# Adding the last chunk's window sums part by part, with parts of 6, 6 and 1 tiles

## The chip, the cores and the metric

The kernel runs on one core of one Trainium2 chip. The metric is the device time of one execution in microseconds (us). Before the change the median of three runs is 8771.89 us (8764.04 to 8781.84).

## The reference

Four graph layers are applied one after the other to 6250 nodes with 128 features. The graph has 206250 edges, sorted by target. Each layer ends in `x = layernorm(x + layer(x))`. Cut to what matters here:

```python
# layer 0: an MLP on each edge, mean over the edges of a target
messages = relu(concat(x[src], x[dst], edge_attr) @ W1 + b1) @ W2 + b2
agg = segment_sum(messages, dst) / clip(counts, 1)

# layers 1, 2, 3: attention over the edges of a target
e = leaky_relu(a_s[src] + a_d[dst], 0.2)
p = exp(e - segment_max(e, dst)[dst])
z = segment_sum(p, dst)
out = segment_sum(h[src] * (p / z[dst]), dst)
# 1: self loops added, skip product, an inner layernorm; 2: plain
# 3: batch norm over all nodes, relu, residual
```

## The kernel before

**Tiles and chunks.** Edges are cut into tiles of 128 and chunks of K = 13 tiles; there are CH = 124 chunks, taken in 62 pairs with two buffers. A layer is an edge stage (all chunks) and then a node stage (13 blocks of up to 512 nodes), which writes the table of rows that the next layer gathers. After the last edge stage comes a final stage of two passes with the batch norm between them.

**A chunk, engine by engine.** Each engine has its own instruction order, written out by hand, with semaphores between them.

- GpSimd (POOL) issues 13 indirect DMAs (L563), one per tile, that gather source rows into `G`. It runs up to two chunks ahead: the gathers of chunk c+2 need the messages of chunk c, since they reuse its buffer.
- VectorE (DVE) starts its part of chunk c with `make_membership` for chunk c+1 (L1172): 0/1 matrices `memb` that say which edge of a tile has which target, formed in three instructions, for the tiles of `PARTED = [(0, 6), (6, 11), (11, 13)]`. Part p waits until TensorE has finished the window sums of the same part of chunk c-1, whose `memb` buffer it overwrites (`summed[p]`). Then, in an attention layer, come a forward scan for segment maxima (L1283, needs the gathered scores through TensorE's L763), window numbers loaded into registers, `keep_factor` (L1232), a backward scan (L1289), `rescale` of the accumulator (L1240, L1242), and the additions of chunk c-1's seven groups of window sums into `acc` (`add_sums`, L1252) in three batches: groups 0 to 2, then 3 and 4 behind L1320, then 5 and 6 behind L1341. Between them lie the carries (L1299 to L1307), the factor (L1313 to L1320), the maxima (L1326, L1328), the softened scores (L1337) and the difference (L1339). The last instruction is the message product (L1345).
- ScalarE (ACT) copies scores (L921), turned membership and so on, and takes the exponential of the difference (L989).
- TensorE (PE) turns `memb` of the next chunk (L699), forms the scores of the next chunk (L756, its first 8 tiles between the carries L777 and the transposition of weights L787, the rest after it), and at the end of the chunk the window sums (L709): for each of 13 tiles one product `memb` x `msg`, two tiles to a group, two TensorE instructions to a product. In layer 1 it also turns the first maxima (L785), which ScalarE copies ahead of the exponential.

In layer 0 a chunk has only the membership, the seven additions, and four additions of pre-activations to gathered rows (L1265); ScalarE applies the relu.

**The end of a layer.** The last chunk has no next membership. `finish_edges` waits for all its sums, rescales and adds the seven groups. TensorE, ScalarE, GpSimd and SyncE (SP) wait for the last of these additions before their node stage. SP's queue then issues, in this order, three loads of node rows (L454), the first two chunks' indices and marks of the next layer (L374, L424, L426), and in layer 0 the store and the reload of the flags of nodes with edges (L491, L493), which TensorE multiplies in L821. The node rows lie in `memb`'s memory.

**Node stages.** VectorE's order is by slots t = -3 to 16; a step with lateness d works on block t-d. In layer 2's node stage and in the final stage the sums of weights are inverted first, for all 49 tiles of nodes at once, 8 heads each (`inverse_weights`: two additions L1395 and L1396, a clamp L1447 or L1449, a reciprocal L1450); each block then uses its share (L1400, L1401, L1456). Layer 1's node stage does a like thing in the two parts of `PARTS`: 16 tiles of nodes first and 33 at slot 1 (`own_scores`, `own_shares`, with the reciprocal L1439).

Of the kernel before, what the change touches and what calls it, by code (L numbers as in the profile page):

```python
# [5 lines left out]
def gnn_program(nc, A, out):  # L6
# [13 lines left out]
    ALU = mybir.AluOpType  # L20
# [26 lines left out]
    HALF = 8  # L47
    PARTED = [(0, 6), (6, 11), (11, K)]
    BIG = float(2 ** 100)
# [7 lines left out]
    with ctx:  # L57
# [286 lines left out]
        def past(l, c):  # L344

            return 2 + CH * l + c
# [7 lines left out]
        def _(sp):  # L354
# [119 lines left out]
            def node_stage(l):  # L474
                sp.wait_ge(added[GR - 1], past(l, CH - 1))
                if l == 0:
# [52 lines left out]
        def _(pool):  # L529
# [91 lines left out]
            for l in range(4):  # L621
                if l:
                    pool.wait_ge(added[GR - 1], past(l - 1, CH - 1))
                    node_stage(l - 1)
                    for r in range(2):
                        pool.wait_ge(stored[r], 16 * len(range(r, NS * l, 2)))
                    for r in range(3):
                        pool.wait_ge(xnew_stored[r], 16 * len(range(r, NS * min(l, 2), 3)))
                else:
                    for k in range(4):  # L630
                        pool.wait_ge(row0_stored[k], 16 * len(range(k, NS, 4)))
                for b in range(2):
                    edges(l, b, b, 0, early=True)
                with pool.Fori(0, PAIRS - 1) as i:
                    for b in range(2):
                        edges(l, 2 * i + 2 + b, b, i + 1)
# [497 lines left out]
        def _(dve):  # L1134
# [140 lines left out]
            def attention(l, c, b, h, prev=True, ahead=True):  # L1275
# [14 lines left out]
                if prev:  # L1290
                    dve.wait_ge(summed[2], past(l, c - 1))
                    rescale(l, c - 1, win)
                    add_sums(l, c - 1, win, 0, 3)

# [26 lines left out]
                if prev:  # L1321
                    add_sums(l, c - 1, win, 3, 5)

# [18 lines left out]
                if prev:  # L1342
                    add_sums(l, c - 1, win, 5, GR)
                dve.wait_ge(wgt_turned, gpast(l, c))
# [11 lines left out]
            def finish_edges(l):  # L1356
                win = window_numbers(CH - 1)
                dve.wait_ge(summed[2], past(l, CH - 1))
                if l:
                    keep_factor(l, CH - 1)  # L1360
                    rescale(l, CH - 1, win)
                add_sums(l, CH - 1, win, 0, GR)
                dve.wait_ge(added[GR - 1], past(l, CH - 1))
# [3 lines left out]
            def then(ins):  # L1367
                count[0] += 1
                ins.then_inc(nvec, 1)
                dve.wait_ge(nvec, count[0])  # L1370
# [33 lines left out]
            def by_head(a):  # L1404
                return a.rearrange("p (j h) -> p j h", h=H)
# [37 lines left out]

            def inverse_weights(add, least):
                all_sums(by_head(zsum), F, 0, NBLK, FW)
                if add:
                    then(ts(zsum, zsum, add, least, ALU.add, ALU.max))  # L1447
                else:
                    then(ts(zsum, zsum, least, None, ALU.max))  # L1449
                then(nc.vector.reciprocal(zsum, zsum))  # L1450

# [71 lines left out]
            def node_stage(l):  # L1523
# [5 lines left out]
                if l == 2:  # L1529
                    inverse_weights(0, 1e-30)  # L1530
                for t in SLOTS:
                    if l == 1 and t == 1:
                        own_scores(1)
                        own_shares(1)
                    s = at(t, 0)
                    g = NS * l + t
# [65 lines left out]

            inverse_weights(1e-16, 1e-30)
            for t in SLOTS:
                s = at(t, -2)
                if s is not None:
# [80 lines left out]
```

## Time and profile before

| | |
|---|---|
| median of 3 runs | 8771.89 us |
| the profiled execution | 8773.27 us |
| its span (first to last instruction) | 8771.2 us |
| TensorE / VectorE / ScalarE / GpSimd busy | 73% / 59% / 24% / 71% of the span |
| granted TensorE clock, mean | 0.828 |
| HBM | 598.03 MB read, 26.58 MB written, 71 GB/s |

The edge stage of layer 0 runs up to 2132 us, that of layer 1 from 2267 to 4363, of layer 2 from 4511 to 6557 and of layer 3 from 6642 to 8688; the node stages lie between them. In the rows, names in brackets after "idle before" say what ended an idle time. "Busy" of TensorE is that of its products; its weight loads (PEld) run beside them. A clock of 1.00 is 2.4 GHz, 0.50 is 1.2 GHz.

### The profile page before, as it was taken

The page shows a single profiled execution, that of the slowest core. Times are in us where ns is not written, and L with a number is a line of the kernel's source. Part 1 is how long each engine was busy: PE and PEld are TensorE (multiplying, and loading weights), DVE is VectorE, ACT ScalarE, POOL GpSimd, SP SyncE. Part 2 cuts the span into 40 slices and gives each one's busy share as a digit, 9 for nine tenths or more (in the row PEclk, how much of TensorE's full clock was granted, in tenths as well). Part 3 has the DMA queues.
Part 4 walks back from the last instruction along what each step waited for, and adds up shares of the span by engine and source line. Part 5 has one row for each costly group of instructions (what it writes and reads, how often), then busy time and mean ns, then how long its engine had stood idle before and what let it go on. Part 6 is the DMA issues. An engine that isn't in the chain of part 4 may idle for free.

```text
span 8771.2 us, 141279 instructions
## 1 busy us (share of the span) xinstructions
PE 6428.0 (73%) x41611; PEld 5776.8 (66%) x41612; DVE 5143.8 (59%) x13620; ACT 2062.1 (24%) x7255; POOL 6267.6 (71%) x6594
## 2 busy tenths in 40 slices
PE   5777777777677777777777777777766777777775
PEld 4777777776566666666656666666655666666664
DVE  3333333334766666666676666666666666666666
ACT  2222222222322222222132222222222222222222
POOL 4777777776677777777657777777765777777774
PEclk7888888888888888888768888888877888888886
DMA  3333333332322222222232222222222222222222
GB/s 101 78 80 78 80 78 80 78 80 66 77 68 68 68 67 66 67 67 68 65 80 69 69 70 69 70 69 70 69 62 73 69 69 69 69 69 69 69 70 50
DMA packets 425473, 625.68 MB, mean 71 GB/s; under 512 B 189634, under 2 KB 305617, under 8 KB 425293
## 3 DMA queue, kind: packets, MB, share of 16 engines
q0 software_dynamic: 206336, 462.61, 22.5%
q1 hardware_dynamic: 219086, 162.49, 7.0%
q8 instruction: 20, 0.33, 0.0%
q14 instruction: 31, 0.25, 0.0%
HBM read 598.03 MB, written 26.58 MB: 71 GB/s over the span
## 4 chain that ended last, share of the span: by engine, by line
POOL 42%; issue 23%; PE 16%; DVE 11%; DMA 4%; DVEq 2%; SPq 1%; ACT 1%; POOLq 0%; ACTq 0%
POOL G L563 41%; PE ps L756 6%; PE ps L709 5%; DMA G<-rows,idx 3%; DVE msg L1345 2%; DVE acc L1252 2%; DVEq L1226 1%; DVE memb L1172 1%; PE ps L728 1%; PE ps L731 1%; PE ps L777 1%; DVE acc L1242 1%; DVE shared L1299 1%; DVE shared L1307 1%; DMA idx<-in_src 1%
## 5 line engine op out<-in xcount | busy, mean ns | idle before, releaser
L563 POOL DMA_INDIRECT G<-rows,idx x6448 | 6126.2, 950 | 2132.6 <-issue 1922.6
L756 PE MATMUL ps<-membT,shared 128*104 128x128 f32 x9672 | 1867.2, 370 | 2.2 <-ACT membT L921 2.2
L709 PE MATMUL ps<-msg,memb 128*128 128x136 f32 (+2 forms) x12896 | 1706.3, 291 | 101.3 <-DVE msg L1345 98.0
L756 PEld LDWEIGHTS ps<-membT,shared 128*104 128x104 f32 x9672 | 1705.6, 248 | 20.1 <-issue 3.0
L709 PEld LDWEIGHTS ps<-msg,memb 128*128 128x128 f32 x12896 | 1623.7, 199 | 128.0 <-issue 66.8
L1172 DVE TENSOR_TENSOR memb<-rel,ps 128x768 f32<-128x768 f32 x1488 | 1044.2, 730 | 1096.2 <-PE ps L709 1094.3
L1252 DVE TENSOR_TENSOR acc<-acc,ps 128x136 f32 (+2 forms) x3472 | 1024.5, 295 | 558.4 <-DVE acc L1252 347.1
L699 PE MATMUL ps<-ident,memb 128*128 128x128 f32 x6448 | 991.5, 292 | 153.8 <-DVE memb L1172 98.4
L728 PE MATMUL ps<-shared,membT 128*128 x3224 | 742.5, 317 | 493.3 <-DVE msg L1265 447.1
L921 ACT ACTIVATE membT<-ps 128x512 f32<-128x512 f32 x1984 | 948.0, 505 | 56.8 <-PE ps L699 52.8
L699 PEld LDWEIGHTS ps<-ident,memb 128*128 128x128 f32 x6448 | 768.9, 149 | 286.4 <-issue 183.0
L728 PEld LDWEIGHTS ps<-shared,membT 128*128 128x128 f32 x3224 | 577.5, 224 | 539.5 <-issue 539.5
L1345 DVE TENSOR_TENSOR msg<-G,ps 128x1768 f32<-128x1768 f32 x372 | 742.6, 1996 | 256.2 <-PE ps L787 253.5
L1265 DVE TENSOR_TENSOR msg<-G,ps 128x512 f32<-128x512 f32 x496 | 280.5, 586 | 767.2 <-PE ps L731 427.9
L731 PE MATMUL ps<-w1e,shared 128*128 128x128 f32 x3224 | 716.4, 309 | 0.0
L777 PE MATMUL ps<-ones,shared 1*104 1x1 f32 x1488 | 239.1, 261 | 601.2 <-DVE shared L1307 601.0
L921 ACT ACTIVATE shared<-G 128x104 f32<-128x104 f32 x372 | 140.5, 378 | 2260.2 <-DMA G<-rows,idx 2260.2
L777 PEld LDWEIGHTS ps<-ones,shared 1*104 1x104 f32 x1488 | 218.2, 217 | 682.7 <-DVE ps L1304 682.7
L958 ACT ACTIVATE msg<-msg 128x512 f32<-128x512 f32 x496 | 268.0, 549 | 1547.1 <-DVE msg L1265 1546.4
L731 PEld LDWEIGHTS ps<-w1e,shared 128*128 128x128 f32 x3224 | 581.6, 225 | 0.0
L768 PE MATMUL ps<-ident,shared 104*1 104x104 f32 x1488 | 204.5, 262 | 408.1 <-DVE shared L1289 407.8
L921 ACT ACTIVATE shared<-shared 128x8 f32 x2604 | 344.1, 216 | 495.9 <-issue 494.1
(182 smaller groups left out, 4552.6 us busy)
## 6 DMA issues: line engine op xcount, KB each, us to landing
G<-rows,idx POOLq DMA_INDIRECT x6448
shared<-marks_all SPq DMA_DIRECT2D x372, 156.0 KB
shared<-in_edge_attr SPq DMA_DIRECT2D x124, 256.0 KB
shared<-in_edge_attr SPq DMA_DIRECT2D x124, 160.0 KB
rows<-msg SPq DMA_DIRECT2D x36, 288.0 KB, 2.7
idx<-in_src SPq DMA_DIRECT2D x496, 6.5 KB
xrows<-msg SPq DMA_DIRECT2D x24, 256.0 KB, 2.2
memb<-xrows SPq DMA_DIRECT2D x24, 256.0 KB, 3.2
```

The lines of the kernel that those rows point to most:

```text
L563: nc.gpsimd.indirect_dma_start(G[:, b, t, 0:rows[l].shape[1]], None, rows[l], bass.IndirectOffsetOnAxis(idx[:, b, t:t + 1], 0)).then_inc(g ...
L699: last = nc.tensor.transpose(ps_mT[j % 2][:, o:o + P], memb[:, b, k * P:(k + 1) * P], ident[:, :])
L709: last = mm(ps_sum[k // 2][:, 0:width], memb[:, b, k * P:(k + 1) * P], msg[:, b, k, 0:width], start=k % 2 == 0, stop=k % 2 == 1 or k == K - 1)
L728: mm(o, membT[:, k, :], btab[:, bass.ds(win[k // 2], 1), :].rearrange("p o f -> p (o f)"), start=True, stop=False)
L731: last = mm(o, ef[:, b, (k - h * HALF) * P:(k - h * HALF + 1) * P], w1e[:, h, :], start=False, stop=True)
L756: last = mm(ps_sc[b][0:JH, :], adz[:, k // 2, K - 1 - k:K - 1 - k + JH], membT[:, k, :], start=k == 0, stop=False)
L777: last = mm(ps_col[0:JH, w:w + 1], carry[0:1, w * JH:(w + 1) * JH], ones[0:1, 0:1], start=True, stop=True)
L921: return nc.scalar.activation(dst, src, ACT.Copy)
L1172: last = tt(memb[:, b, k0 * P:k1 * P].rearrange("p (k n) -> p k n", k=n), r, w, ALU.is_equal)
L1252: tt(a, a, ps_sum[g][:, 0:width], ALU.add).then_inc(added[g], 1)
L1265: o = tt(msg[:, b, k0:k1, 0:P], G[:, b, k0:k1, 0:P], ps_pre[j % 2][:, 0:(k1 - k0) * P].rearrange("p (k f) -> p k f", k=k1 - k0), ALU.add)
L1345: tt(msg[:, b, :, 0:MW].rearrange("p k (h f) -> p k h f", h=H), G[:, b, :, 0:MW].rearrange("p k (h f) -> p k h f", h=H), ps_wgt.rearrange( ...
```

## The change

The parts become 6, 6 and 1 tiles. VectorE's additions wait for the sums of their own part, in three batches of groups 0 to 2, 3 to 5 and 6, in the loop and at the end of a layer; factor and rescale no longer wait for the sums. SP and GpSimd go into the node stage when the last sums are done, not when they are added. `inverse_weights` works on one part of the nodes: the first at the stage's head, the second at slot 1 of layer 2's node stage and at slot 0 of the final stage.

```diff
-    PARTED = [(0, 6), (6, 11), (11, K)]
+    PARTED = [(0, 6), (6, 12), (12, K)]
...
             def node_stage(l):
-                sp.wait_ge(added[GR - 1], past(l, CH - 1))
+                sp.wait_ge(summed[2], past(l, CH - 1))
...
                 if l:
-                    pool.wait_ge(added[GR - 1], past(l - 1, CH - 1))
+                    pool.wait_ge(summed[2], past(l - 1, CH - 1))
...
                 if prev:
-                    dve.wait_ge(summed[2], past(l, c - 1))
                     rescale(l, c - 1, win)
+                    dve.wait_ge(summed[0], past(l, c - 1))
                     add_sums(l, c - 1, win, 0, 3)
...
                 if prev:
-                    add_sums(l, c - 1, win, 3, 5)
+                    dve.wait_ge(summed[1], past(l, c - 1))
+                    add_sums(l, c - 1, win, 3, 6)
...
                 if prev:
-                    add_sums(l, c - 1, win, 5, GR)
+                    dve.wait_ge(summed[2], past(l, c - 1))
+                    add_sums(l, c - 1, win, 6, GR)
...
             def finish_edges(l):
                 win = window_numbers(CH - 1)
-                dve.wait_ge(summed[2], past(l, CH - 1))
                 if l:
                     keep_factor(l, CH - 1)
                     rescale(l, CH - 1, win)
-                add_sums(l, CH - 1, win, 0, GR)
+
+                for p, (g0, g1) in enumerate(((0, 3), (3, 6), (6, GR))):
+                    dve.wait_ge(summed[p], past(l, CH - 1))
+                    add_sums(l, CH - 1, win, g0, g1)
                 dve.wait_ge(added[GR - 1], past(l, CH - 1))
...
-            def inverse_weights(add, least):
-                all_sums(by_head(zsum), F, 0, NBLK, FW)
+            def inverse_weights(add, least, part):
+                j0, j1 = PARTS[part]
+                z = zsum[:, j0 * H:j1 * H]
+                all_sums(by_head(z), F, j0, j1, FW)
                 if add:
-                    then(ts(zsum, zsum, add, least, ALU.add, ALU.max))
+                    then(ts(z, z, add, least, ALU.add, ALU.max))
                 else:
-                    then(ts(zsum, zsum, least, None, ALU.max))
-                then(nc.vector.reciprocal(zsum, zsum))
+                    then(ts(z, z, least, None, ALU.max))
+                then(nc.vector.reciprocal(z, z))
...
                 if l == 2:
-                    inverse_weights(0, 1e-30)
+                    inverse_weights(0, 1e-30, 0)
                 for t in SLOTS:
...
+                    if l == 2 and t == 1:
+                        inverse_weights(0, 1e-30, 1)
...
-            inverse_weights(1e-16, 1e-30)
+            inverse_weights(1e-16, 1e-30, 0)
             for t in SLOTS:
+                if t == 0:
+                    inverse_weights(1e-16, 1e-30, 1)
```

## Rows read from the trace of the kernel before

**Rows 1.** The page: the chain that ended last, and the gathers' group.
```profile
POOL 42%; issue 23%; PE 16%; DVE 11%; DMA 4%; DVEq 2%; SPq 1%; ACT 1%; POOLq 0%; ACTq 0%
...
L563 POOL DMA_INDIRECT G<-rows,idx x6448 | 6126.2, 950 | 2132.6 <-issue 1922.6
```

**Rows 2.** Layer 2: L1345 (ns min/median/max, first to last start), then waits (us, times, longest).
```profile
L1345 DVE TENSOR_TENSOR msg<-G,ps x124: 1995/1996/1998, 4536.7 to 6545.6; 128x1768 f32<-128x1768 f32 x124
...
POOL G L563 <- DVE msg L1345: 4.9, 16, 0.3
...
DVE shared L1283 <- PE ps L763: 69.0, 75, 5.8
```

**Rows 3.** Layer 1: L1345, and the waits of GpSimd and VectorE.
```profile
L1345 DVE TENSOR_TENSOR msg<-G,ps x124: 1995/1997/1998, 2295.1 to 4351.2; 128x1768 f32<-128x1768 f32 x124
...
POOL G L563 <- DVE msg L1345: 58.8, 62, 2.8
...
DVE msg L1345 <- PE ps L787: 88.3, 93, 2.5
DVE acc L1252 <- DVE acc L1252: 76.0, 492, 0.2
...
DVE shared L1283 <- PE ps L763: 5.7, 5, 3.9
```

**Rows 4.** Layer 0: a wait of VectorE.
```profile
DVE msg L1265 <- DMA G<-rows,idx: 334.3, 120, 4.4
```

**Rows 5.** Timeline of VectorE in layer 1 (start, duration us, engine, line).
```profile
4308.81 0.95 DVE L1172 TENSOR_TENSOR memb<-rel,ps 128x768 f32<-128x768 f32 x1 [3.26 <-PE ps L709]
4310.03 1.15 DVE L1172 TENSOR_TENSOR memb<-rel,ps 128x640 f32<-128x640 f32 x2 [0.27 <-PE ps L709]
4311.10 0.41 DVE L1283 TENSOR_TENSOR_SCAN shared<-shared,ps 104x128 f32<-104x128 f32 x1
...
4316.91 0.35 DVE L1326 SCALAR_TENSOR_TENSOR shared<-shared,ps 104x128 f32<-104x128 f32 x1
...
4318.48 0.29 DVE L1339 TENSOR_TENSOR shared<-shared 104x128 f32<-104x128 f32 x1
...
4319.20 0.30 DVE L1252 TENSOR_TENSOR acc<-acc,ps 128x144 f32 x1 [0.15 <-DVE acc L1252]
4319.52 2.00 DVE L1345 TENSOR_TENSOR msg<-G,ps 128x1768 f32<-128x1768 f32 x1
```

**Rows 6.** Timelines of VectorE, SP and TensorE after layer 0's last sums.
```profile
2129.88 0.29 DVE L1252 TENSOR_TENSOR acc<-acc,ps 128x129 f32 x1 [2.74 <-PE ps L709]
...
2132.87 2.20 SPq L454 DMA_DIRECT2D memb<-in_x_rows  x3
...
2138.57 0.28 SPq L491 DMA_DIRECT2D flags<-shared  x1
...
2144.25 2.07 PE L821 MATMUL ps<-shared,b_u 1*128 1x512 f32 x2 [3.62 <-DMA shared<-flags]
```

**Rows 7.** Timelines of TensorE and VectorE at the end of layer 1.
```profile
4353.28 6.16 PE L709 MATMUL ps<-msg,memb 128*128 128x144 f32 x26 [1.55 <-DVE msg L1345]
...
4359.48 0.17 DVE L1232 TENSOR_SCALAR shared<-ps 128x16 f32<-128x16 f32 x1 [6.25 <-PE ps L709]
...
4363.28 0.30 DVE L1252 TENSOR_TENSOR acc<-acc,ps 128x144 f32 x1 [0.15 <-DVE acc L1252]
```

**Rows 8.** Timeline of VectorE: the inverse weights of layer 2's node stage, and what follows.
```profile
6557.83 0.84 DVE L1395 TENSOR_TENSOR shared<-acc 64x392 f32<-64x392 f32 x1
...
6559.94 2.60 DVE L1450 RECIPROCAL shared<-shared 128x392 f32<-128x392 f32 x1
6562.57 0.72 DVE L1400 TENSOR_TENSOR acc<-acc 64x544 f32<-64x544 f32 x1
```

**Rows 9.** The line of the reciprocal in layer 1's node stage.
```profile
L1439 DVE RECIPROCAL shared<-shared x2: 954/1380/1805, 4368.4 to 4394.8; 128x128 f32<-128x128 f32 x1, 128x264 f32<-128x264 f32 x1
```

**Rows 10.** TensorE in two stretches of layer 1: us, busy (instructions), clock, DMA share, GB/s.
```profile
4011.00:4017.50 6.50, 3.52 (x28) 1.00 0.24 58
4017.50:4024.00 6.50, 5.95 (x27) 0.50 0.33 82
```

## The prediction

> **What bounds the kernel now.** I read the page first: the chain that ended last spends 42% of the span on GpSimd and 23% on "issue", mostly the gap before each gather [rows 1]. A gather takes 950 ns and some 300 ns pass before the next (1922.6 us over 6300) [rows 1], so 13 gathers cost about 16.2 us, and no chunk of 13 tiles can be shorter. Whether a layer runs at that pace is a question for each layer, so I took the waits by layer next.
>
> In layers 2 and 3 the gathers set the pace. Layer 2's 124 message products start between 4536.7 and 6545.6 us, so one chunk takes 2008.9/123 = 16.33 us; GpSimd waited for messages 4.9 us in all, while the first scan (L1283) waited 69.0 us, in 75 chunks, for the scores that follow a gather [rows 2]. That is 0.56 us a chunk by which VectorE arrives too early. Layer 3 gives nearly the same in both views.
>
> Layer 1 is different. Its messages start from 2295.1 to 4351.2 us: 2056.1/123 = 16.72 us a chunk. GpSimd waited 58.8 us, 62 times, for them, and L1283 waited for scores in only 5 chunks [rows 3]. Here no gather is late; a loop over VectorE and TensorE sets the pace: window sums on TensorE, membership of the next chunk on VectorE, scans, the scores' differences, exponential on ScalarE, transposition on TensorE, messages, sums again. Every delay on that loop is paid 123 times.
>
> Layer 0 has room: its message additions wait 334.3 us, 120 times, for the gathers themselves, 2.8 us each [rows 4].
>
> **Edit 1: parts of 6, 6 and 1 tiles.** Elements and instruction count stay the same; what moves is when part 1 may start. It now waits for the sums of 12 tiles in place of 11. The timeline shows that this wait is live: part 0 starts at 4308.81, released by TensorE, ends after 0.95 us, VectorE idles 0.27 us, and parts 1 and 2 start at 4310.03 and take 1.15 us together, with the scan right behind at 4311.10 [rows 5]. Part 0 starts after tile 6 and part 1 after tile 11, so five tiles took 1.22 us: 0.24 us a tile. Part 1 starts 0.24 us later, parts 1 and 2 are still seven tiles and still 1.15 us, so memb is ready 0.24 us later, and the scan and TensorE's turning of memb with it. In layer 1: 123 x 0.24 = 30 us. From below, nothing, if the scan turned out to wait for something else; the 5 waits in 123 chunks speak against it. From above 0.48 us a tile, 59 us: at the layer's end, with a slow TensorE, 26 products (13 tiles) take 6.16 us [rows 7]. I take 30, the row inside the loop. In layers 2 and 3 the scan has its 0.56 us; in layer 0 its 2.8 us.
>
> **Edit 2: the sixth group's add is moved** from behind L1341 to before L1326. One add follows another at 0.46 us (the first that moves starts at 4319.20, 0.44 after the one before; L1252 waits 0.15 us for its predecessor each time) [rows 5, 3]. VectorE goes straight from the adds to L1326 at 4316.91, so L1326 to L1339 all come 0.46 us later, and ScalarE's exponential waits for L1339. Behind it one add fewer stands before the message product. Where VectorE is last, that isn't a swap for nothing: from the end of L1339 (4318.77) to the message (4319.52) lie 0.75 us, filled by L1341 and two adds, and the exponential, transposition and their hand-overs need about the same time. So the message slips by the whole 0.46. Where TensorE is last (its 16 score products stand before the transposition), it slips less or not at all: in 93 of the chunks of layer 1 the message waited for L787, 88.3 us in total, 0.95 each [rows 3]. Going through layer 1 chunk by chunk, the gap from the end of L1339 to the start of the exponential is under 0.06 us in 32 of 121 chunks, over 0.46 in 57, and between in 32; the mean slip is 0.16 us. 123 x 0.16 = 20 us; the ends are 0 and 0.46 x 123 = 57 us. In layers 2 and 3 the same reading gives 0.15 and 0.13 us. With edit 1 that is 0.4 us a chunk against 0.56 of room, on average but not in every chunk, so I add 1 us for both.
>
> **Edit 3: new waits for the sums.** In the loop they are all met already, since the membership at the chunk's head waited for the same sums. Two more waits stand in VectorE's queue in each chunk of layers 1 to 3; an address step of that queue is 0.07 us in the chain. Taking them at nothing is my choice (the queue runs ahead while an instruction is busy); at 0.07 each layer 1 would pay up to 17 us.
>
> **Edit 4: the last chunk.** VectorE idles 6.25 us for all 26 products, then does L1232, the rescale and seven adds, the last starting at 4363.28 and ending at 4363.58 [rows 7]. Now L1232 and the rescale (1.0 us) run during the sums, and so do adds 0 to 2. TensorE ends at 4359.44, tile 12 about 0.47 earlier; adds 3, 4, 5 and 6 then follow from 4359.0 and end at 4359.0 + 3 x 0.46 + 0.30 = 4360.7. Gain 2.9 us in layer 1, and as VectorE's first work of the node stage depends on it, it is a gain of the path. Layers 2 and 3 gain 2.7 each by the same sum with 0.45 spacing. In layer 0 no rescale stands there, and the adds alone would give 1.6.
>
> **Edit 5: row loads released by the sums.** In layer 0's node stage SP's own queue is the path: it starts at 2132.87, behind the last add, issues three row loads and the next layer's indices and marks, and only then stores the flags at 2138.57; TensorE, waiting for them, goes on at 2144.25 [rows 6]. The sums were done about 2129.8, just before the first add at 2129.88 [rows 6], so everything in that queue starts 3.0 us earlier; the flags themselves are ready 1.6 us earlier, at about 2133.7, in time for the new 2135.5. Gain 3.0 us there, in place of edit 4's 1.6. In the other stages VectorE's own sums come first, and rows that land earlier give nothing. GpSimd's earlier release gives nothing either: its first work waits for rows or VectorE.
>
> **Edit 6: inverse weights in two parts.** Before, L1395 to L1450 take from 6557.83 to 6562.57, 4.74 us, 2.60 of it the reciprocal [rows 8]. In two parts I price by layer 1's equal shapes: the reciprocal of 128 columns is 0.95, of 264 columns 1.80 [rows 9]; with sums and the clamp about 2.04 + 3.34 = 5.38 us. The first rows start 2.7 us earlier, but the second part is then paid in the middle. VectorE is the busy engine of both stages (in the last one its instructions follow each other without idle up to the batch's statistics), so the net is a loss of 0.6 us, twice: 1.3 us. If other engines limited these stages, it would be a gain of up to 2.7 each.
>
> **Sum.** Against the profiled execution's own 8773.27 us (span 8771.2 and 2.1 around it; it lies 1.4 above the median 8771.89): +30 +20 +1 -2.9 -2.7 -2.7 -3.0 +1.3 = +41, so 8814 us.
>
> **Rivals.**
> A. *The loop swallows both shifts, and only the ends remain* (not slower). Layer 1 is just 0.39 us a chunk above the gathers' 16.33, and its messages already wait 88.3 us for TensorE. If the later membership and the later difference both fall into waits for TensorE's score products, 8773.3 - 10 = 8763. It decides if layer 1 stays at 16.72 or below. Against it: the scan waits for scores in only 5 of 123 chunks [rows 3], and the later difference is hidden in half of the chunks, not in all.
> B. *TensorE's clock adds to it, and layers 2 and 3 lose their room.* In layer 1 the granted clock stood at 1.00 (2.4 GHz) in a stretch in which TensorE was busy 3.52 of 6.5 us, and at 0.50 (1.2 GHz) in the 6.5 us after that [rows 10]. The change lengthens the thin stretch between sums and score products by 0.24 us. If this costs 0.2 us more a chunk, layer 1 pays 25 more, and layers 2 and 3, with 0.4 + 0.2 against 0.56, some 5 to 10 each: about 8850. Against it: a chunk that comes later may as well fall where the clock is high.
> The Trainium skill, "TensorE: Matmul & The Clock Gate", section "Part 1: The HAM clock gate", says that the throttled half-rate clock is the resting state, that sustained activity lifts it and idleness brings it back. By that rule each longer thin stretch speaks against the change, as in B; the rows above agree in direction, and none shows the price of 0.24 us.
> C. *Edit 1 alone counts*, as the add is hidden: 8773.3 + 30 + 1 - 10 = 8794, at the lower end of my forecast's own range.
>
> **How the numbers follow.** A measurement of this kernel tells 0.2%, 17.5 us, from no change. Forecast with C inside it 0.72 (own range 8790 to 8840), A 0.15, B 0.13. The range goes from 8768, which leaves out most of A, to 8856, which takes in the middle of B. Slower by over 0.2%: 0.67 of the forecast's 0.72, and all of B: 0.80. Within 0.2%: most of A and the forecast's low end, 0.16. Faster: 0.04, only if layer 1's loop gets shorter by luck with the clock.
>
> **What would show it.** Right: layer 1's messages 17.1 us apart, GpSimd's wait for them at 90 to 110 us, part 1 of memb preceded by 0.5 us of idle, L1339 0.46 later behind L1320; layers 2 and 3 still 16.33 apart, with L1283's wait for scores down from 69 us to about 35; the flags' store 3 us earlier behind the last gather. Wrong: layer 1 at 16.72, or layers 2 and 3 above 16.4.

## The result and the profile after

| | median us (range) | profiled execution / span | granted clock |
|---|---|---|---|
| before, 6 runs beside it | 8776.86 (8764.04 to 8791.08) | 8773.27 / 8771.2 | 0.828 |
| after, 6 runs | 8810.07 (8805.74 to 8820.36) | 8805.74 / 8804.0 | 0.837 |

The ratio is 1.0039, with an interval of 1.0026 to 1.0052: the change makes the kernel 33 us slower, by the medians and by the two spans alike. Forecast were 41 us. The total came out, but the experiments below show that it is partly a cancellation: one large term of the sum is nothing, the other is twice its size, and layers 2 and 3 take 8.6 us more where 1 us was forecast.

The page after, the rows that answer to [rows 1]: the chain that ended last has the same shares, and the gathers the same busy time, while the idle time before them grew by 36 us.
```profile
POOL 41%; issue 23%; PE 17%; DVE 12%; DVEq 2%; DMA 2%; ACT 1%; SPq 1%; POOLq 0%; ACTq 0%
...
L563 POOL DMA_INDIRECT G<-rows,idx x6448 | 6126.2, 950 | 2168.5 <-issue 1924.0
```

Layer by layer it goes by the message product, which is L1347 now. Layer 1 and layer 2 after (ns min/median/max, first to last start), the rows that answer to [rows 3] and [rows 2]:
```profile
L1347 DVE TENSOR_TENSOR msg<-G,ps x124: 1995/1996/1998, 2289.2 to 4382.9; 128x1768 f32<-128x1768 f32 x124
...
L1347 DVE TENSOR_TENSOR msg<-G,ps x124: 1995/1996/1998, 4565.9 to 6579.0; 128x1768 f32<-128x1768 f32 x124
```
Layer 1 takes 2093.7/123 = 17.02 us a chunk, against 16.72: 37.6 us more in all. Layer 2 takes 2013.1/123 = 16.37, against 16.33: 4.2 us more, and layer 3 as much. The waits of the same two layers (us in total, times, longest): VectorE in layer 1 up to 4346 us, which is 121 chunks, then GpSimd in the whole of layer 1, then VectorE in layer 2:
```profile
DVE msg L1347 <- PE ps L787: 106.0, 117, 1.8
...
DVE shared L1232 <- issue: 78.1, 121, 1.4
```
```profile
POOL G L563 <- DVE msg L1347: 101.9, 69, 3.4
```
```profile
DVE shared L1283 <- PE ps L763: 20.9, 36, 5.2
```
In layer 1 the messages now wait for the transposition of weights (L787) in 117 of 121 chunks, where they did in 93 of 123, and GpSimd waits 101.9 us for messages instead of 58.8. In layer 2 the scan's wait for scores, VectorE's room there, is down from 69.0 us to 20.9.

A chunk of layer 1 after, on VectorE (start, duration us):
```profile
3313.19 0.95 DVE L1172 TENSOR_TENSOR memb<-rel,ps 128x768 f32<-128x768 f32 x1 [3.34 <-PE ps L709]
3314.66 1.15 DVE L1172 TENSOR_TENSOR memb<-rel,ps 128x768 f32<-128x768 f32 x2 [0.51 <-PE ps L709]
3315.72 0.41 DVE L1283 TENSOR_TENSOR_SCAN shared<-shared,ps 104x128 f32<-104x128 f32 x1
3316.32 0.17 DVE L1232 TENSOR_SCALAR shared<-ps 128x16 f32<-128x16 f32 x1 [0.18 <-issue]
...
3321.75 0.30 DVE L1252 TENSOR_TENSOR acc<-acc,ps 128x144 f32 x1 [0.15 <-DVE acc L1252]
3321.97 0.35 DVE L1327 SCALAR_TENSOR_TENSOR shared<-shared,ps 104x128 f32<-104x128 f32 x1
...
3323.53 0.29 DVE L1340 TENSOR_TENSOR shared<-shared 104x128 f32<-104x128 f32 x1
...
3323.82 0.28 DVE L1252 TENSOR_TENSOR acc<-acc,ps 128x144 f32 x1
3324.57 2.00 DVE L1347 TENSOR_TENSOR msg<-G,ps 128x1768 f32<-128x1768 f32 x1 [0.47 <-PE ps L787]
```
Against [rows 5], part 1 of `memb` is preceded by 0.51 us of idle and not 0.27, as forecast. Behind the difference (L1340) stands one add and not two, and then VectorE idles 0.47 us for L787, where [rows 5], one of the 30 chunks before the change whose message did not wait for L787, has no idle at all: the message waits for what the difference released.

The time between layers, from the last to the first message product, in us:

| kernel | layer 0's last gather to layer 1 | layer 1, a chunk | to layer 2 | layer 2, a chunk | to layer 3 | layer 3, a chunk | last message to the end |
|---|---|---|---|---|---|---|---|
| before | 176.8 | 16.716 | 185.5 | 16.333 | 124.1 | 16.323 | 93.8 |
| after | 173.5 | 17.022 | 183.0 | 16.367 | 119.9 | 16.359 | 93.0 |
| e8_parts661 | 173.0 | 16.711 | 184.4 | 16.298 | 124.1 | 16.282 | 94.6 |
| e9_add_moved | 173.1 | 17.054 | 185.5 | 16.299 | 121.4 | 16.298 | 93.7 |
| e7_best | 171.3 | 16.415 | 184.7 | 16.378 | 119.2 | 16.395 | 92.0 |
| e10_hoist | 173.0 | 16.354 | 185.5 | 16.340 | 123.6 | 16.323 | 93.7 |

The changed kernel: +37.6 in layer 1, +4.2 and +4.4 in layers 2 and 3, and 3.3 + 2.5 + 4.2 + 0.8 = 10.8 back between the layers. That makes 35.4 us, where the spans differ by 32.8; the rest, -2.6, lies in layer 0, whose last gather starts that much earlier.

### The profile page after: what moved, and what is told of

Its sections match the earlier page's. It is cut to its first block, busy times and chain, and to the rows that moved or that the text cites. A ratio compares the mean times of both kernels' runs of the same rounds, so it can differ in the third digit from the quotient of the medians.

```text
span 8804.0 us, 142220 instructions
## 1 busy us (share of the span) xinstructions
PE 6417.0 (73%) x41611; PEld 5734.1 (65%) x41612; DVE 5141.2 (58%) x13628; ACT 2080.9 (24%) x7255; POOL 6266.9 (71%) x6594
## 4 chain that ended last, share of the span: by engine, by line
POOL 41%; issue 23%; PE 17%; DVE 12%; DVEq 2%; DMA 2%; ACT 1%; SPq 1%; POOLq 0%; ACTq 0%
POOL G L563 40%; PE ps L709 7%; PE ps L756 6%; DVE msg L1347 2%; DVE acc L1252 2%; DMA G<-rows,idx 2%; DVEq L1226 1%; PE ps L728 1%; PE ps L731 1%; DVE acc L1242 1%; PE ps L777 1%; DVE shared L1299 1%; PE ps L787 1%; DVE shared L1307 1%; DVEq L1252 1%
## 5 line engine op out<-in xcount | busy, mean ns | idle before, releaser
L709 PE MATMUL ps<-msg,memb 128*128 128x136 f32 (+2 forms) x12896 | 1778.9, 300 | 110.3 <-DVE msg L1347 109.4
L756 PE MATMUL ps<-membT,shared 128*104 128x128 f32 x9672 | 1784.5, 358 | 2.3 <-ACT membT L921 2.3
L709 PEld LDWEIGHTS ps<-msg,memb 128*128 128x128 f32 x12896 | 1695.7, 207 | 136.0 <-issue 73.4
L756 PEld LDWEIGHTS ps<-membT,shared 128*104 128x104 f32 x9672 | 1607.7, 236 | 26.8 <-issue 3.0
L1347 DVE TENSOR_TENSOR msg<-G,ps 128x1768 f32<-128x1768 f32 x372 | 742.6, 1996 | 283.7 <-PE ps L787 281.7
L768 PE MATMUL ps<-ident,shared 104*1 104x104 f32 x1488 | 198.6, 257 | 275.5 <-DVE shared L1289 275.0
```

The costliest lines, as they stand in the source:

```text
L709: last = mm(ps_sum[k // 2][:, 0:width], memb[:, b, k * P:(k + 1) * P], msg[:, b, k, 0:width], start=k % 2 == 0, stop=k % 2 == 1 or k == K - 1)
L756: last = mm(ps_sc[b][0:JH, :], adz[:, k // 2, K - 1 - k:K - 1 - k + JH], membT[:, k, :], start=k == 0, stop=False)
L1347: tt(msg[:, b, :, 0:MW].rearrange("p k (h f) -> p k h f", h=H), G[:, b, :, 0:MW].rearrange("p k (h f) -> p k h f", h=H), ps_wgt.rearrange( ...
```

## The experiments

Each is an edit of the kernel before, if nothing else is said, and each is compared with runs of the kernel before on the same chip. They fall into two groups. In one, the kernel before takes 8.77 ms, as in the profile; in the other the same program takes 12.8 to 13.1 ms. The chips of the first group are numbered 0, 4, 8 and 12 in the record, those of the second 3, 4, 11 and 15; number 4 stands in both, so whether the chip makes the difference isn't shown. Only the first group can speak for the change. I give it first.

**e8_parts661: edit 1 alone.**
```diff
-    PARTED = [(0, 6), (6, 11), (11, K)]
+    PARTED = [(0, 6), (6, 12), (12, K)]
```


> The kernel before with the parts 6, 6, 1 and nothing else, a third time: the first two ran on chips where the kernel before took 12.8 and 13.1 ms. After the whole change layer 1 stands at 17.02 us a chunk, +0.31 where my two terms sum to +0.40. If this kernel runs at 8.8 ms: my term says 16.96 in layer 1 (+30 us); if the terms overlap, each alone may give up to +0.31. The rival that the loop swallows the later membership: 16.72, +0. The rival of the clock: 17.07 or more, as TensorE is cold in more chunks.

8757.41 us against 8765.62, ratio 0.9988 (0.9977 to 0.9999). Layer 1 stays at 16.71 us a chunk (2055.4 us, against 2056.1). The later membership costs nothing, where I had put 30 us. Its timeline, and its waits in layer 1:
```profile
3301.83 0.95 DVE L1172 TENSOR_TENSOR memb<-rel,ps 128x768 f32<-128x768 f32 x1 [3.15 <-PE ps L709]
3303.30 1.15 DVE L1172 TENSOR_TENSOR memb<-rel,ps 128x768 f32<-128x768 f32 x2 [0.51 <-PE ps L709]
3304.37 0.41 DVE L1283 TENSOR_TENSOR_SCAN shared<-shared,ps 104x128 f32<-104x128 f32 x1
3304.95 0.17 DVE L1232 TENSOR_SCALAR shared<-ps 128x16 f32<-128x16 f32 x1 [0.18 <-issue]
```
```profile
DVE msg L1345 <- PE ps L787: 86.8, 84, 2.7
...
DVE shared L1232 <- issue: 80.5, 123, 1.3
```
The kernel before, in the same stretch, and its waits in layer 1:
```profile
3301.96 0.95 DVE L1172 TENSOR_TENSOR memb<-rel,ps 128x768 f32<-128x768 f32 x1 [3.17 <-PE ps L709]
3303.18 1.15 DVE L1172 TENSOR_TENSOR memb<-rel,ps 128x640 f32<-128x640 f32 x2 [0.27 <-PE ps L709]
3304.25 0.41 DVE L1283 TENSOR_TENSOR_SCAN shared<-shared,ps 104x128 f32<-104x128 f32 x1
3305.09 0.18 DVE L1232 TENSOR_SCALAR shared<-ps 128x16 f32<-128x16 f32 x1 [0.42 <-issue]
```
```profile
DVE shared L1232 <- issue: 110.3, 123, 1.4
```
And the loads of the window numbers on VectorE's queue in that layer (ns min/median/max, first to last start):
```profile
L1226 DVEq TENSOR_LOAD <-jtab x123: 1034/1624/1639, 2302.0 to 4342.0; - x123
```
The membership indeed ends 0.25 us later behind the start of part 0 (2.29 and 2.54 us to the scan). But L1232 starts 3.13 us behind part 0 before the change and 3.12 in e8. Before L1232 VectorE idles for its own queue, which is reading the window numbers into registers: in this chunk the load starts at 3304.0 before the change and takes 1.04 us, and L1232 follows at 3305.09; in e8 it starts at 3303.9 and takes 1.03 us, and L1232 follows at 3304.95. Counted from part 0 the load starts after 2.04 us in both, so the parts don't move it. The whole layer says the same: in the median of the 123 chunks the load starts 2.05 us behind part 0 and L1232 3.72 us behind it in both kernels, and L1232 starts 0.05 us behind the end of the load in every chunk. The idle shrinks from 0.42 to 0.18 us, over the layer from 110.3 to 80.5 us. The 30 us that I had charged to the path are exactly these.

**e9_add_moved: edit 2 alone.**
```diff
-                    add_sums(l, c - 1, win, 3, 5)
+                    add_sums(l, c - 1, win, 3, 6)
...
-                    add_sums(l, c - 1, win, 5, GR)
+                    add_sums(l, c - 1, win, 6, GR)
```


> The kernel before with only the sixth group's addition moved ahead of the maxima, a third time. e8_parts661 at 8.8 ms left layer 1 at 16.71 us a chunk: the later membership costs nothing, since VectorE idles anyway before L1232, for its window numbers. So layer 1's +0.31 of the whole change has to come from the additions. New theory: this kernel alone gives layer 1 at 17.0 (+0.3, +35 us) and layers 2 and 3 at 16.36; my first term was 0.16 a chunk, 16.88 and +20 us, and then the two waits that the change adds to VectorE's queue would hold the rest.

8792.53 us against 8769.3, ratio 1.0026 (1.0015 to 1.0037). Layer 1 takes 17.05 us a chunk, 0.34 more, 41 us in the layer; 2.7 us less lie in the stage before layer 3, and layers 2 and 3 take 4.1 and 3.1 us less, which is why the medians differ by 23 us only. So this one edit by itself makes the whole loss of layer 1. The changed kernel's 17.02 is no more than it, so its two further waits a chunk (edit 3) and the later membership add nothing that shows in layer 1; no run has edit 3 alone. Its waits in layer 1 up to 4340 us:
```profile
DVE shared L1232 <- issue: 106.1, 119, 1.4
...
DVE msg L1345 <- PE ps L787: 105.1, 120, 1.9
```
The idle before L1232 is what it was before; the messages' wait is that of the changed kernel. In this profile the granted clock in layer 1 was 0.79, against 0.84 in the changed kernel's, at the same pace of chunks; over the whole run it was 0.80, and the seven other executions of e9, at 0.83, took 8782.72 to 8796.12 us, so the loss is there at the usual clock too.

**e10_hoist: the window numbers read ahead of the membership.** If the idle before L1232 is VectorE's own queue, reading the registers earlier must give it back.
```diff
             def attention(l, c, b, h, prev=True, ahead=True):
+                if prev:
+                    win = window_numbers(c - 1)
                 if ahead:
                     make_membership(l, c + 1, 1 - b)
...
                 if prev:
-                    win = window_numbers(c - 1)
                     keep_factor(l, c - 1)
```


> The kernel before with one thing moved: VectorE reads the window numbers into its registers ahead of the membership instructions, in place of behind the first scan. What e8_parts661 leaves to explain is why a membership that ends 0.24 us later costs nothing. My theory: the register loads (DVEq L1226, followed by an idle named issue, 0.9 us a chunk before L1232 in layer 1) run from the moment the queue has passed the wait for the last sums, beside the membership instructions, and end after them. If so, taking them out of the way lets L1232 follow the scan at once, and layer 1 falls from 16.72 to the gathers' 16.30 to 16.33 us a chunk, up to -50 us. Rival: L1232 waits for TensorE's factor (fac_out) or something else, its idle stays at 0.9 us and the time at 8770.

8722.59 us against 8765.53, ratio 0.9945 (0.9927 to 0.9964): the fastest version. Layer 1 takes 16.35 us a chunk, the gathers' pace. A stretch of its timeline, then its waits in layer 1 (lines moved by one or two), and its chain of waits on the page:
```profile
3309.84 0.42 DVE L1285 TENSOR_TENSOR_SCAN shared<-shared,ps 104x128 f32<-104x128 f32 x1 [1.87 <-PE ps L763]
3310.18 0.15 DVE L1232 TENSOR_SCALAR shared<-ps 128x16 f32<-128x16 f32 x1
```
```profile
DVE shared L1285 <- PE ps L763: 143.1, 101, 7.3
...
DVE msg L1346 <- PE ps L787: 57.0, 41, 1.9
```
```profile
POOL 54%; issue 25%; DVE 8%; PE 6%; DMA 5%; SPq 1%; ACT 1%; DVEq 0%; ACTq 0%; POOLq 0%
```
L1232 stands right behind the scan, with no idle. VectorE now comes early and the scan waits for the scores in 101 chunks, where it did in 5 [rows 3]. DVEq, VectorE's queue, is gone from the chain that ended last, and GpSimd has 54% of it, against 42% [rows 1]. The idle that hid edit 1 was thus on the path, and worth 123 x 0.36 = 45 us of its 110.3 before the gathers set the pace.

**e7_best: the ends (edits 4 and 5), with other parts and other batches.** The last chunk's adds go bank by bank, by a semaphore of their own for the second PSUM bank; SP and GpSimd wait for the sums; the inverse stays whole; parts are 6, 4 and 3 tiles and batches 1, 3 and 3.
```diff
-    PARTED = [(0, 6), (6, 11), (11, K)]
+    PARTED = [(0, 6), (6, 10), (10, K)]
+        second_bank = chunk_sem("window_sums_of_second_bank_ready")
...
-                sp.wait_ge(added[GR - 1], past(l, CH - 1))
+                sp.wait_ge(summed[2], past(l, CH - 1))
...
-                    pool.wait_ge(added[GR - 1], past(l - 1, CH - 1))
+                    pool.wait_ge(summed[2], past(l - 1, CH - 1))
...
+                    if k == 11:
+                        last.then_inc(second_bank, 1)
...
-                    add_sums(l, c - 1, win, 0, 3)
+                    add_sums(l, c - 1, win, 0, 1)
...
-                    add_sums(l, c - 1, win, 3, 5)
+                    add_sums(l, c - 1, win, 1, 4)
...
-                    add_sums(l, c - 1, win, 5, GR)
+                    add_sums(l, c - 1, win, 4, GR)
...
-                dve.wait_ge(summed[2], past(l, CH - 1))
...
-                add_sums(l, CH - 1, win, 0, GR)
+                for done_sums, g0, g1 in ((summed[0], 0, 3), (second_bank, 3, 6), (summed[2], 6, GR)):
+                    dve.wait_ge(done_sums, past(l, CH - 1))
+                    add_sums(l, CH - 1, win, g0, g1)
```


> A version meant to beat both: the ends of the change (groups added bank by bank, SP and GpSimd released by the last sums), the inverse weights left whole, parts of 6, 4 and 3 tiles in place of 6, 5 and 2, and the seven additions of a chunk in batches of 1, 3 and 3 in place of 3, 2 and 2. On a chip where the kernel before takes 8.8 ms: the parts let the last membership instruction end 0.12 us earlier, and two additions fewer stand before the carries, so that TensorE's score products start 0.9 us earlier; layer 1 then falls from 16.72 to the gathers' 16.33 us a chunk, -47 us, and the ends give -11: 8718 us, ratio 0.993. Rival: the carries wait for TensorE's maxima instead, layer 1 stays at 16.7, and only -11 remains. On a chip like the last two (12.8 to 13.1 ms) every layer is bound by TensorE's late results, and I expect -1% from the ends, as e3_ends showed, and at most 1% more.

8739.78 us against 8772.5, ratio 0.9963 (0.995 to 0.9975). Layer 1 falls to 16.42 us a chunk. Its chunks differ in several things at once: one add fewer stands ahead of the difference (the opposite of edit 2), two fewer ahead of the carries, and part 1 of the membership waits for 10 tiles, not 11. No run tells them apart. Layers 2 and 3 rise by 0.05 and 0.07 us a chunk, and the time is 22 us above the 8718 I expected. The split inverse can be compared too: e7's two last stages, with the inverse whole, take 119.2 and 92.0 us, the changed kernel's 119.9 and 93.0.

**The runs of the second group.** Edit 1 alone, edit 2 alone, the ends alone (parts 6, 5 and 2, batches as before), the inverse alone, edits 1 and 2 again; then e10's edit with e3's, and e10's edit with the whole change. The edits of e1, e2, e5 and e6 are those shown above for e8 and e9; e3 is e7 without its changes of `PARTED` and of the batches in the loop; e4 is the change's `inverse_weights` with its calls.

> The kernel before with the parts 6, 6, 1 and nothing else. My theory (edit 1 is paid in layer 1 only): in layer 1 the second part of memb starts 0.24 us later in each of 123 chunks, so messages stand about 16.96 us apart in place of 16.72, +30 us in all, 8803 against 8773. The rival that the loop swallows it: layer 1 stays at 16.72, time within 5 us of before. The rival of the clock: more than 0.35 us a chunk in layer 1, +45 or more.

> The kernel before with only the sixth group's addition moved ahead of the maxima, behind the fifth. My theory: the difference comes 0.46 us later in each chunk, which a chunk pays in full where VectorE is last and not at all where TensorE is: 0.16 us a chunk in layer 1, +20 us. Rival: the add is swapped for nothing, +0 to 3 us. Upper rival: every chunk pays the 0.46, +57 us.

> The kernel before with the parts 6, 5, 2 kept and only the ends changed: last chunk's groups added bank by bank (a semaphore of its own for the second bank), SP and GpSimd released by the last sums. My theory: -3.0 us at layer 0's end by SP's queue, -2.9, -2.7 and -2.7 at the others, -11 us in all, too little for the timed runs to tell but to be read in the profile's stages. Rival: each end is hidden behind another engine, 0.

> The kernel before with only the inverse weights in two parts. My theory: 0.6 us lost in layer 2's node stage and 0.6 us in the final one, since VectorE is the busy engine of both. Rival: up to 2.7 us won in each, as the first block's rows start 2.7 us earlier.

> The kernel before with the parts 6, 6, 1 and nothing else, again, since the first time the kernel before itself took 13.1 ms on that chip and no layer there was paced by its gathers. If it runs at 8.8 ms here: my theory, layer 1's messages 16.96 us apart in place of 16.72, +30 us; the rival that the loop swallows it, 16.72; the rival of the clock, 17.07 or more.

> The kernel before with only the sixth group's addition moved ahead of the maxima, again for the same reason. My theory: 0.16 us a chunk in layer 1, +20 us, messages 16.88 us apart. From the profile after the whole change (layer 1 at 17.02, +0.31 in place of the +0.40 of my two terms) the two shifts overlap, so that each alone may cost up to its term and both together less. Rival: the add costs nothing, and the whole +0.31 belongs to the parts.

> The version meant to beat both: the window numbers read ahead of the membership as in e10_hoist, parts and batches of additions as before the change, and of the change only the ends (groups added bank by bank, SP and GpSimd released by the last sums), inverse weights whole. e10_hoist gave -43 us against before, the ends were worth -11 by my terms and -10.8 in the change's own profile with the split inverse weights in it: 8712 us, ratio 0.9935. Rival: with layer 1 at the gathers' pace the ends are hidden behind the table's stores, 8722.

> The whole change, with the window numbers read ahead of the membership. In it the later difference cost layer 1 its +0.31 us a chunk, as every microsecond on that loop was paid. In e10_hoist L1283 waits for scores 143 us in layer 1, 1.2 us a chunk. If that room is what was missing, the change's parts and additions cost nothing here: layer 1 at 16.35, and with the ends the kernel comes to 8715 us. Rival: they use up the room in part, layers 1 to 3 at 16.4 to 16.5 and 8735 us or more.

| kernel | median us | before, same chip | ratio (interval) |
|---|---|---|---|
| e1_parts661 | 13104.37 | 13118.65 | 0.9986 (0.9972 to 1.0) |
| e2_add_moved | 13112.31 | 13118.65 | 1.0000 (0.9987 to 1.0012) |
| e3_ends | 12958.44 | 13118.65 | 0.9898 (0.9869 to 0.9927) |
| e4_inverse | 13134.65 | 13118.65 | one run |
| e5_parts661 | 12790.97 | 12804.02 | 0.9993 (0.9975 to 1.0012) |
| e6_add_moved | 12820.32 | 12804.02 | 1.0016 (0.9998 to 1.0034) |
| e11_hoist_ends | 12716.36 | 12921.0 | 0.9834 (0.9813 to 0.9854) |
| e12_after_hoist | 12812.87 | 12976.04 | 0.9873 (0.9853 to 0.9894) |

They don't test the forecast, because no layer is paced there as in its profile. The chain of e1's page, and two of its waits over the whole run:
```profile
another core or an unknown queue 31%; PE 28%; DVE 19%; issue 15%; DVEq 5%; ACT 1%; POOL 1%; SPq 1%; DMA 0%; ACTq 0%; POOLq 0%
```
```profile
POOL G L563 <- DVE msg L1345: 3384.4, 366, 12.5
...
DVE shared L1299 <- remote: 2110.8, 356, 15.6
```
GpSimd waits for the messages in nearly every chunk of the attention layers, 366 of 372. What the directions say: edit 1 is again nothing, edit 2 nothing or slightly slower, and the ends gain 1.0%, far more than in the first group. Hoist and ends together (0.9834) come out ahead of hoist and the whole change (0.9873), on different chips and with intervals that touch. Neither pair ran in the first group, so whether the ends add to e10's 8722.59 us is open.

## Why the prediction was right in sum and wrong in some of its steps

- **Bounds.** Right. Layers 2 and 3 go by the gathers, layer 1 by a loop over VectorE and TensorE: a delay of one add costs 41.5 us in layer 1 and none in the other two (e9).
- **Edit 1, +30: wrong, measured 0** (e8). The step that failed is "memb is ready 0.24 us later, and the scan and TensorE's turning of memb with it. In layer 1: 123 x 0.24 = 30 us". Up to the scan it holds. But the path doesn't go on from the scan: L1232 waits for VectorE's queue, which reads the window numbers, and this read starts 2.05 us behind part 0 in both kernels. As I read it, it starts when the queue has passed its wait for the last tile's sums, which the new parts don't move. The later membership was taken out of 110.3 us of idle that already lay behind it. I had argued only that the scan waits for no scores; I should have asked what the next instruction waits for. Of the views behind [rows 3], the same list of waits had this row, "DVE shared L1232 <- issue", 110.3 us in 123 chunks. Shown by e8 and, from the other side, by e10.
- **Edit 2, +20: right in mechanism, half its size, measured +38 to +41** (after: 37.6; e9: 41.5). The term that was mis-sized is "the mean slip is 0.16 us". I took the slack of each chunk as it stood in the kernel before, and averaged what would stick out of 0.46 us. In the kernel after, the exponential starts less than 0.06 us behind the difference in 63 of the 124 chunks, and in e9 in 91, where by the same count it was 31 before (the prediction has 32 of 121); the message waits for L787 in nearly all chunks, where it did in 93 of 123. With the difference later, it is the last to arrive far more often, and most of the 0.46 that I had named as the upper end is paid. How much stays open: 0.46 us in each of those chunks would be an estimated 42 us for e9, which took 41.5, but 29 for the changed kernel, which took 37.6. The pattern of slack shifts with the whole chunk, and I have no run that fixes it.
- **Layers 2 and 3, +1: measured +8.6, most of it not by waiting.** The room was used as forecast: the scan's wait for scores falls from 69.0 to 20.9 us, 0.39 us a chunk, which is the prediction's 0.4. Its "about 35" is a slip, since 69.0 - 123 x 0.39 is 21. The two terms of the 0.4 were both off: alone, edit 1 takes 0.16 a chunk (48.8 us are left in e8) and edit 2 takes 0.27 (36.2 in e9), where I had 0.24 and 0.15. For edit 2 the kernel before had a row that I overlooked; in layer 2 the exponential (L989) waits for the difference in every chunk, so by my rule none had any slack there:
```profile
ACT shared L989 <- DVE shared L1339: 198.3, 123, 2.1
```
  What failed is the step from the room to the time ("0.4 us a chunk against 0.56 of room, on average but not in every chunk, so I add 1 us for both"). GpSimd's busy time (the second number of its row) in layer 2, before and after, and then its waits in the same order:
```profile
4536.70:6545.60 2008.90, 1511.95 (x1592) 0.83 0.29 69
...
4565.90:6579.00 2013.10, 1514.30 (x1592) 0.85 0.28 69
```
```profile
POOL G L563 <- issue: 480.3, 1576, 0.3
...
POOL G L563 <- issue: 481.9, 1581, 0.4
POOL G L563 <- DVE msg L1347: 4.5, 11, 1.4
```
  GpSimd doesn't wait longer for messages: 4.5 us against 4.9 [rows 2], and 2.1 against 5.2 in layer 3. Both waits together grow by 1.2 us in layer 2 and 0.5 in layer 3, near the 1 us forecast. Most of the rest lies in the gathers themselves, which are busy 2.4 and 4.0 us longer. That busy time differs between kernels anyway: in layer 2 it is 4.3 and 4.5 us below that of the kernel before in e8 and e9, and 1.9 and 5.7 above it in e10 and e7, with the same waits to within 1 us. Whether the change makes gathers longer or profiles differ by that much isn't shown.
- **Edit 3 at nothing: not contradicted.** The changed kernel, with two more waits, is no slower in layer 1 than e9 without them. No run has them alone.
- **Edits 4 and 5: right at the ends of layers 1 to 3, not at layer 0's.** The stages' gains are 10.8 us net against the kernel before, forecast -10.0. At layer 1's end the message starts at 4382.93 and the last add ends at 4392.89, 9.96 us; before it was 4351.22 to 4363.58, 12.36 us, so -2.4 for the 2.9 that I had put. VectorE after, where [rows 7] has the seven adds behind one wait:
```profile
4384.84 0.17 DVE L1232 TENSOR_SCALAR shared<-ps 128x16 f32<-128x16 f32 x1
...
4388.39 0.30 DVE L1252 TENSOR_TENSOR acc<-acc,ps 128x144 f32 x1 [2.66 <-PE ps L709]
...
4391.14 0.30 DVE L1252 TENSOR_TENSOR acc<-acc,ps 128x144 f32 x1 [1.53 <-PE ps L709]
...
4392.59 0.30 DVE L1252 TENSOR_TENSOR acc<-acc,ps 128x144 f32 x1 [0.22 <-DVE acc L1252]
```
  The rescale and three adds lie in TensorE's sums, as said. In layer 0's node stage, SP's queue after (what answers to [rows 6]):
```profile
2127.39 1.50 SPq L454 DMA_DIRECT2D memb<-in_x_rows  x3
...
2132.80 0.28 SPq L491 DMA_DIRECT2D flags<-shared  x1
```
  The flags' store comes 17.1 us behind the last gather (2115.7) and before 20.3 us (2138.57 - 2118.3): 3.2 earlier, forecast 3.0. But of this only 1.2 us reach TensorE, which takes the flags in L821: 24.8 us behind the last gather after (2140.45), 26.0 before, and 25.2 to 25.6 in e8, e9 and e10, which have the old code there. The row loads, released earlier, also let GpSimd start earlier (L575, which waits for them), and now it runs beside VectorE's first two additions on `acc`, whose block TensorE's L808 waits for. First the kernel before, then after:
```profile
2134.24 0.68 DVE L1400 TENSOR_TENSOR acc<-acc 64x512 f32<-64x512 f32 x1
...
2136.66 1.41 POOL L575 TENSOR_TENSOR memb<-memb,reps 128x512 f32<-128x512 f32 x1 [17.38 <-DMA memb<-in_x_rows]
```
```profile
2130.51 1.26 POOL L575 TENSOR_TENSOR memb<-memb,reps 128x512 f32<-128x512 f32 x1 [13.84 <-DMA memb<-in_x_rows]
...
2131.76 1.77 DVE L1404 TENSOR_TENSOR acc<-acc 64x512 f32<-64x512 f32 x1
```
  The two take 1.77 and 1.66 us after, 0.68 and 0.69 before; e7, which has the same edit, shows 1.77 and 1.66 too. That rows which land earlier start GpSimd earlier, beside VectorE, is a price that the prediction didn't have. The stage as a whole shows no gain: it takes 173.5 us after, and 173.0 to 173.1 in e8, e9 and e10; only against the 176.8 of the kernel before is it 3.3 shorter. Kernels that share a stage differ in it by up to 4 us. Against the mean of all four kernels that have the stages' old code, the four stages of the changed kernel are 7 us shorter, not 10.8.
- **Edit 6, +0.6 twice: its parts as priced, its net not resolved.** VectorE after, in layer 2's node stage, for the rows of [rows 8]:
```profile
6589.21 0.95 DVE L1456 RECIPROCAL shared<-shared 128x128 f32<-128x128 f32 x1
6590.20 0.72 DVE L1404 TENSOR_TENSOR acc<-acc 64x544 f32<-64x544 f32 x1
...
6598.23 0.62 DVE L1399 TENSOR_TENSOR shared<-acc 64x264 f32<-64x264 f32 x1
...
6599.83 1.81 DVE L1456 RECIPROCAL shared<-shared 128x264 f32<-128x264 f32 x1
```
  The two parts take 2.05 and 3.44 us, together 5.49 against 4.74 (forecast 5.38). Against e7 the stages are 0.7 and 1.0 us longer, which fits the 0.6 but lies within what such stages scatter.
- **Rivals.** A, that the loop swallows both shifts, is half true, for the membership alone. B fell: layer 1's clock was 0.84 before and 0.84 after, and layers 2 and 3 had 0.83 before and 0.85 after, so the loss did not come with a lower clock. C had the wrong edit: one of the two counts alone, but it is the add.

So the forecast's -10 was about right (-7 to -11), and +30 + 20 + 1 = 51 comes near the 0 + 37.6 + 8.6 = 46 of the runs only because the errors of -30, +18 and +8 nearly cancel. That the total came out is luck. The mark "layer 1's messages 17.1 us apart" was met (17.02) and proved nothing about how the 0.3 us is shared out between the two edits.

## What to carry to other kernels

Before a delay is charged to a loop, follow it over the next two instructions and look at what each of them already waits for: the idle put down to "issue" was here the engine's own queue at work (register reads); it hid a delay that arrived in front of it, and it was itself worth removing (45 us, more than the change cost). An operation moved ahead of a hand-over to another engine cost most of its own time here (0.34 of 0.46 us), whatever slack the chunks showed on average before. Before a longer layer is charged to a wait, see whether the wait grew or the busy time of the engine that sets the pace. And a total that comes out says nothing about its terms: run the two largest alone.

## What the runs showed of the hardware

Reading the seven window numbers of one chunk holds VectorE's queue for 1.62 us at the median (L1226 above), nearly as long as its message product is busy (2.00 us), and VectorE's busy time shows none of it. Placed ahead of a wait that is long anyway (2.0 us before the membership at the median of e10's chunks in layer 1) it costs nothing that shows.

VectorE's operations on two tensors in SBUF took longer while GpSimd worked on two tensors as well. Alone, L1400 takes 0.68 us (64x512, the kernel before at 2134.24); beside GpSimd's L575 and L593 the same addition (L1404 after) takes 1.77 us. VectorE's reciprocal, which reads one tensor, takes 0.47 us beside L575 (after, at 2130.67) as it does alone (before, at 2133.62).

The same program takes 8.77 ms in some executions and 12.8 to 13.1 ms in others, far more apart than the change makes, with granted clocks of 0.83 and about 0.71. In e1's trace VectorE goes on late behind TensorE: L768's product ends at 5504.9 us and L1299, which needs it, starts at 5509.58 (such idle of L1299 is put down to "remote", 2110.8 us in 356 waits, 5.9 each). What holds these executions back isn't settled by these runs; all that they can say is what two kernels measured on the same chip say of each other.
